# Norm, split and logits of three batches made during the last batch of attention

## The reference, cut to what matters

```
h = layernorm(x)                              # no weights
y = h + attn(layernorm(h, ln1_w, ln1_b))      # conv, q/k/v, rope, 16 heads, causal softmax, proj
z = layernorm(y, ln2_w, ln2_b)
expert = argmax(z @ router_w)                 # one of 4
out = y + (silu(z @ Wg[expert]) * (z @ Wv[expert])) @ proj[expert]
x = x + 0.5 * out
```

## Time and profile before

| | us |
|---|---|
| runs, median (lowest to highest) | 2196.71 (2192.24 to 2207.43), 3 runs |
| the profiled execution | 2191.62 |
| its span in the trace | 2189.9 |
| PE, DVE, ACT, POOL busy | 1866.5, 1437.3, 1302.0, 581.3 |

### The profile page before, as it was taken

The page is one execution under the profiler, slowest core; times in us unless marked ns, Lnnn a source line. Parts: engine busy times, 40 slices in busy tenths (PEclk is TensorE's granted clock), DMA queues, the critical chain, the costliest instruction groups (busy, mean ns, idle before and its releaser), DMA issues.

```text
span 2189.9 us, 23815 instructions
## 1 busy us (share of the span) xinstructions
PE 1866.5 (85%) x8305; PEld 1056.7 (48%) x8324; DVE 1437.3 (66%) x2318; ACT 1302.0 (59%) x2022; POOL 581.3 (27%) x685
## 2 busy tenths in 40 slices
PE   8999999999999989998677777997677677777998
PEld 6886444344434437885233334784122323332786
DVE  6886564456445647886755653886899755662787
ACT  6997555555555558997255556555644535556554
POOL 1443000000000002443522222222599612223221
PEclk9999999999999999999689998998799779999999
DMA  3221000000000002220000000200000000000110
GB/s 97 79 69 56 1 17 17 0 17 17 17 0 17 10 10 71 71 73 29 1 1 1 1 1 1 78 29 0 10 3 31 1 1 1 1 1 1 52 55 19
DMA packets 23746, 52.39 MB, mean 24 GB/s; under 512 B 2336, under 2 KB 6816, under 8 KB 23648
## 3 DMA queue, kind: packets, MB, share of 16 engines
q1 hardware_dynamic: 23648, 51.12, 7.3%
HBM read 49.47 MB, written 1.64 MB: 23 GB/s over the span
## 4 chain that ended last, share of the span: by engine, by line
PE 57%; DVE 21%; ACT 14%; issue 4%; POOL 2%; DMA 1%; ACTq 0%; POOLq 0%; DVEq 0%; SPq 0%
PE ps L440 9%; PE ps L442 9%; PE ps L441 9%; PE ps L708 5%; DVE arena L1463 5%; PE ps L225 4%; DVE arena L1208 4%; PE ps L701 4%; PE ps L928 3%; PE ps L898 3%; ACT rstd L242 2%; PE ps L887 2%; ACT arena L990 2%; ACT arena L1040 2%; ACT rstd L238 2%
## 5 line engine op out<-in xcount | busy, mean ns | idle before, releaser
L548 DVE TENSOR_TENSOR hid_lo<-arena,hid_hi 128x512 fp32r<-128x512 f32 x384 | 340.6, 900 | 67.1 <-ACT arena L498 64.7
L526 POOL TENSOR_TENSOR w_lo<-wslot,w_hi 128x512 fp32r<-128x512 f32 x56 | 77.5, 1389 | 759.4 <-DVE w_hi L543 759.4
L1208 DVE TENSOR_REDUCE arena<-ps 128x1 f32<-128x512 f32 (+3 forms) x352 | 213.2, 638 | 88.8 <-PE ps L902 85.7
L440 PE MATMUL ps<-x_hi,w_hi 128*128 128x512 f32 x512 | 208.1, 406 | 0.6 <-DVE arena L630 0.6
L441 PE MATMUL ps<-x_lo,w_hi 128*128 128x512 f32 x512 | 205.2, 401 | 0.0
L442 PE MATMUL ps<-x_hi,w_lo 128*128 128x512 f32 x512 | 205.0, 400 | 0.0
L495 ACT ACTIVATE hid_hi<-ps,wslot 128x512 fp32r<-128x512 f32 x256 | 177.1, 692 | 34.1 <-PE ps L442 6.3
L1040 ACT ACTIVATE arena<-ps 128x1024 f32<-128x1024 f32 (+3 forms) x256 | 166.5, 706 | 48.5 <-PE ps L918 47.9
L1126 POOL TENSOR_SCALAR_AFFINE_SELECT arena<-arena 128x256 f32<-128x256 f32 x256 | 102.2, 406 | 330.7 <-ACT arena L1040 328.2
L898 PE MATMUL ps<-arena 128*128 128x128 bf16 (+3 forms) x498 | 132.5, 332 | 65.3 <-DVE arena L1208 37.1
L498 ACT ACTIVATE arena<-ps,wslot 128x512 f32<-128x512 f32 x256 | 175.1, 684 | 0.0
(11 more groups left out here) (225 smaller groups left out, 3863.7 us busy)
## 6 DMA issues: line engine op xcount, KB each, us to landing
arena<-gates_dram SPq DMA_DIRECT2D x96, 256.0 KB, 3.5
wslot<-pack_a SPq DMA_DIRECT2D x16, 514.5 KB, 3.7
wslot<-pack_b SPq DMA_DIRECT2D x8, 901.5 KB, 4.6
wslot<-pack_c SPq DMA_DIRECT2D x8, 768.0 KB, 4.5
res<-x_in SPq DMA_DIRECT2D x4, 256.0 KB, 4.5
out_dram<-res SPq DMA_DIRECT2D x4, 256.0 KB, 2.9
bc_dram<-arena SPq DMA_DIRECT2D x1, 384.0 KB, 3.2
arena<-bc_dram SPq DMA_DIRECT2D x16, 24.0 KB
```

The lines of the kernel that those rows point to most:

```text
L440: pe.matmul(ps[:, bank, :], w1, hi, start=start, stop=False)
L548: dve.tensor_tensor(hid_lo[item % 2][:, k, :], hid32[:, k, :], hid_hi[item % 2][:, k, :].bitcast(F32), ALU.subtract).then_inc(S["hid_ok"], 1)
L1208: dve.tensor_reduce(neg_max[:, i, heads[0]:heads[-1] + 1:step], ps[:, bank, 0:len(heads) * keys].rearrange("p (m k) -> p m k", k=keys), AX ...
```

## The change

The norm of batches 0, 1 and 2 moves into batch 3 of attention. Each is spread over steps that begin at j = 2, 5 and 8 (`NORM_STEPS`): PE makes the mean behind the scores of step j+1 and the variance one step on; ACT squares behind the exponentials of step j, takes Ln and Exp one step on, and the high part three steps on; DVE centres at j, scales at j+2, and makes the low part at j+4. DVE now makes both parts of the weights of expert 0, at j = 0 to 2; POOL's part of that goes. The router products of batches 0 to 2 stand between the last turns and the last projection, in bank 5, and DVE copies their logits out ahead of the last `added_back`. Batch 3 is normed inside the experts' first item: its mean stands behind unit 0 on PE, its variance behind unit 2, its logits in unit 4, and ACT takes its square, Ln and Exp ahead of the first Silu. The gates are transposed at item 1, k = 3 instead of item 1, k = 0; DVE takes the rest of the router in unit 4 and the copy of the gates in unit 5. The counts of units, of products and of DMAs stay.

```diff
+        LATE = NB - 1
+        NORM_BANKS = [(5, 6)] * LATE + [(6, 7)]
+        EARLY_BANK, LATE_BANK = 5, 7
+        def pe_norm_mean(pe, c, t):
+            n, bank = c["ln"] + 2, NORM_BANKS[t][0]
+            pe.wait_ge(S["t_free"], att_x1(c, t))
+            if 0 < t < LATE:
+                pe.wait_ge(S["ln_xc"], 4 * n + t)
+            pe.matmul(ps[:, bank, :], mean_w, hb[:, t, :], start=True, stop=True).then_inc(S["ln_mean"], 1)
+        def pe_norm_var(pe, c, t):
+            pe.wait_ge(S["ln_sq"], 4 * n + t + 1)
...
+            pe.matmul(ps[:, bank, :], mean_w, sq[:, t, :], start=True, stop=True).then_inc(S["ln_var"], 1)
+        def act_norm_square(act, c, t):
+            act.wait_ge(S["ln_xc"], 4 * (c["ln"] + 2) + t + 1)
+            act.activation(sq[:, t, :], xc[:, t, :], ACT.Square).then_inc(S["ln_sq"], 1)
+        def act_norm_root(act, c, t):
+            act.wait_ge(S["ln_var"], 4 * n + t + 1)
+            act.activation(rstd[:, t, :], ps[:, NORM_BANKS[t][1], :], ACT.Ln, bias=eps).then_inc(S["ln_log"], 1)
+            act.wait_ge(S["ln_log"], 4 * n + t + 1)
+            act.activation(rstd[:, t, :], rstd[:, t, :], ACT.Exp, scale=-0.5).then_inc(S["ln_rs"], 1)
...
@@ dve_router (top == 1)
-                dve.tensor_copy(val, lg).then_inc(S["lg_read"], 1)
+                early = experts * TPB * LATE
+                dve.wait_ge(S["lg_early"], late + 1)
+                dve.tensor_copy(arena[:, 8192:8192 + early], ps[:, EARLY_BANK, 0:early]).then_inc(S["lg_part"], 1)
+                yield
+                dve.wait_ge(S["logits"], call + 1)
+                dve.tensor_copy(arena[:, 8192 + early:8192 + TILES * experts],
+                                ps[:, LATE_BANK, early:TILES * experts]).then_inc(S["lg_read"], 1)
                 dve.wait_ge(S["lg_read"], call + 1)
-                yield
+                dve.wait_ge(S["lg_part"], late + 1)
@@ pe_experts1
-                    if item == 1 and k == 0:
+                    if (item, k) == (0, 0):
+                        pe_norm_mean(pe, c, LATE)
+                    if (item, k) == (0, 2):
+                        pe_norm_var(pe, c, LATE)
+                    if (item, k) == (1, 0):
+                        pe_norm_logits(pe, c, LATE, LATE_BANK).then_inc(S["logits"], 1)
+                    if (item, k) == (1, 3):
                         pe_gates(pe, c["moe_call"], EXPERTS1)
@@ act_experts1
+            act_norm_square(act, c, LATE)
+            act_norm_root(act, c, LATE)
             for n in range(total + 1):
+                if n == 1:
+                    act_norm_high(act, c, LATE)
@@ dve_experts1
-            next(router)
+            dve_norm_centre(dve, c, LATE)
+            dve_norm_scale(dve, c, LATE)
...
-                if n in (0, 6):
+                if n == 2:
+                    dve_norm_low(dve, c, LATE)
+                if n == 4:
+                    next(router)
+                if n in (5, 8):
                     next(router, None)
@@ pe_attention, batch 3 (b + 1 == NB)
+        NORM_STEPS = [2, 5, 8]
+                    else:
+                        if j in NORM_STEPS:
+                            pe_norm_mean(pe, c, NORM_STEPS.index(j))
+                        if j - 1 in NORM_STEPS:
+                            pe_norm_var(pe, c, NORM_STEPS.index(j - 1))
                     values(b, j)
...
-            for m in range(3, TURNS):
-                turned(NB - 1, m)
+            turned(NB - 1, 3)
+            pe_norm_logits(pe, c, 0, EARLY_BANK)
+            turned(NB - 1, 4)
+            pe_norm_logits(pe, c, 1, EARLY_BANK)
+            pe_norm_logits(pe, c, 2, EARLY_BANK).then_inc(S["lg_early"], 1)
+            turned(NB - 1, 5)
@@ act_attention, batch 3
+                        if j in NORM_STEPS:
+                            act_norm_square(act, c, NORM_STEPS.index(j))
+                        if j - 1 in NORM_STEPS:
+                            act_norm_root(act, c, NORM_STEPS.index(j - 1))
+                        if j - 3 in NORM_STEPS:
+                            act_norm_high(act, c, NORM_STEPS.index(j - 3))
@@ dve_attention, batch 3
+                        if j < C_PIECES:
+                            dve_weights(dve, c, C_PIECES, 0, j)
+                        if j in NORM_STEPS:
+                            dve_norm_centre(dve, c, NORM_STEPS.index(j))
+                        if j < C_PIECES:
+                            cut = slice(SEQ * j, SEQ * j + SEQ)
+                            dve.wait_ge(S["w_hi_ok"], c["parts"] + j + 1)
+                            dve.tensor_tensor(w_lo[0][:, cut], wslot[:, 0, cut], w_hi[0][:, cut].bitcast(F32),
+                                              ALU.subtract).then_inc(S["w_parts"], 1)
+                        if j - 2 in NORM_STEPS:
+                            dve_norm_scale(dve, c, NORM_STEPS.index(j - 2))
+                        if j - 4 in NORM_STEPS:
+                            dve_norm_low(dve, c, NORM_STEPS.index(j - 4))
             normed(NB - 1, 3)
+            next(router)
             added_back(NB - 1)
```

More of the change, by code:

```diff
@@ L284, in act_ln_split, with dve_ln_split @@
             split(NB - 1)
-        def dve_ln_split(dve, n, src, affine, c, pieces):
+        def dve_ln_split(dve, n, src, c, pieces):
             for t in range(NB):
@@ L299, in dve_ln_split @@
                 dve.wait_ge(S["ln_rs"], 4 * n + t + 1)
[L300 to L307, removed]
+                dve.tensor_tensor(ha[:, t, :], xc[:, t, :], rstd[:, t, :], ALU.mult).then_inc(S["ln_out"], 1)
                 if t:
@@ new lines, in pe_norm_logits @@
+        def pe_norm_logits(pe, c, t, bank):
+            pe.wait_ge(S["ln_out"], 4 * (c["ln"] + 2) + t + 1)
+            for i in range(TPB * t, TPB * t + TPB):
+                mm = pe.matmul(ps[:, bank, EXPERTS1 * i:EXPERTS1 * (i + 1)], ha[:, t, (i % TPB) * P:(i % TPB + 1) * P],
+                               pcol("router"), start=True, stop=True)
+            return mm
+        def act_norm_square(act, c, t):
+            act.wait_ge(S["ln_xc"], 4 * (c["ln"] + 2) + t + 1)
+            act.activation(sq[:, t, :], xc[:, t, :], ACT.Square).then_inc(S["ln_sq"], 1)
@@ new lines, in act_norm_root, with act_norm_high @@
+        def act_norm_root(act, c, t):
+            n = c["ln"] + 2
+            act.wait_ge(S["ln_var"], 4 * n + t + 1)
+            act.activation(rstd[:, t, :], ps[:, NORM_BANKS[t][1], :], ACT.Ln, bias=eps).then_inc(S["ln_log"], 1)
+            act.wait_ge(S["ln_log"], 4 * n + t + 1)
+            act.activation(rstd[:, t, :], rstd[:, t, :], ACT.Exp, scale=-0.5).then_inc(S["ln_rs"], 1)
+        def act_norm_high(act, c, t):
+            act.wait_ge(S["ln_out"], 4 * (c["ln"] + 2) + t + 1)
+            act.activation(x_hi[:, t, :], ha[:, t, :], ACT.Copy).then_inc(S["x_hi_ok"], 1)
@@ new lines, in dve_norm_centre, with dve_norm_scale @@
+        def dve_norm_centre(dve, c, t):
+            dve.wait_ge(S["ln_mean"], 4 * (c["ln"] + 2) + t + 1)
+            dve.tensor_tensor(xc[:, t, :], hb[:, t, :], ps[:, NORM_BANKS[t][0], :],
+                              ALU.subtract).then_inc(S["ln_xc"], 1)
+        def dve_norm_scale(dve, c, t):
+            n, m = c["ln"] + 2, c["lns"] + 1
+            dve.wait_ge(S["ln_rs"], 4 * n + t + 1)
+            dve.scalar_tensor_tensor(out=ha[:, t, :], in0=xc[:, t, :], scalar=pcol("ln2_w"), in1=rstd[:, t, :],
+                                     op0=ALU.mult, op1=ALU.mult).then_inc(S["ln_scaled"], 1)
+            dve.wait_ge(S["ln_scaled"], 4 * m + t + 1)
+            dve.tensor_scalar(ha[:, t, :], ha[:, t, :], pcol("ln2_b"), None, ALU.add).then_inc(S["ln_out"], 1)
@@ L333, in build, with dve_router @@
         chain = [0]
-        def dve_router(dve, call, exp_call, experts, top):
+        def dve_router(dve, call, exp_call, experts, top, late=0):
             def link(ins):
@@ L347, in dve_router @@
             desc = ccol("desc8" if experts == 8 else "desc4").unsqueeze(1).to_broadcast([P, TILES, experts])
-            dve.wait_ge(S["logits"], call + 1)
-            lg = ps[:, LOGIT_BANK, 0:TILES * experts].rearrange("p (t e) -> p t e", e=experts)
             val = tile3(0)
             if top == 2:
+                dve.wait_ge(S["logits"], call + 1)
+                lg = ps[:, LOGIT_BANK, 0:TILES * experts].rearrange("p (t e) -> p t e", e=experts)
                 link(dve.tensor_reduce(rs[0], lg, AX_X, ALU.max))
@@ L453, in pe_down @@
                     pe.wait_ge(S["gate_cp"], c["moe_call"] + 1)
+                if banks == 2 and item == 0:
+                    pe.wait_ge(S["ln_xc"], 4 * (c["ln"] + 2) + NB)
             pe.wait_ge(S["hid_ok"], 4 * (base + item) + k + 1)
@@ L529, in pool_experts @@
         def pool_experts(pool, c, dst, experts, pieces, lag):
-            pool_weights(pool, c, pieces, 0)
+            if experts == EXPERTS0:
+                pool_weights(pool, c, pieces, 0)
             for item in range(NB * experts + lag):
@@ L1152, in dve_conv, with dve_attention @@
```

(4 more changed lines are left out.)

24 lines of the change are left out of this document (16 added, 8 removed).

## The result

The changed kernel takes 2225.75 us (median of 4 runs, 2223.35 to 2227.82) against 2202.07 us before (4 runs, 2192.24 to 2208.88), a ratio of 1.0111 (95% interval 1.0063 to 1.0158). Forecast were 2206 us and a range of 2188 to 2222. It is slower, on the side that was forecast: by 24 us between these medians, where the prediction had added 12 us to the profiled run.

A forecast was written before the change was run, and what follows sets the result against it. Bound: a serial chain of small pieces, 18.8 us between attention and experts, twice. Per stage +14.5 - 11.9 + 3.4 = +6.0, +12.0 for two, giving 2203.6 from 2191.6; with half of 5.1 us carried, 2206; range 2188 to 2222.

The forecast's parts named there:

- Term 1: Batch 3 of attention gets 14.5 us longer per stage: 18.9 for three norms, less 4.4 of old ACT waits absorbed.
- The bound of 20.2: Upper bound for batch 3's lengthening per stage, if PE is at half clock for each of the six norm products.
- The sign that I gave: What would show the forecast right in batch 3 of attention: it lasts 44 us instead of 29.7.
- Term 2: From the last turn of attention to unit 3 of the experts: 11.9 us shorter per stage.
- my bound: Last turn to unit 3: -10.3 us if the eight later router products also run at half clock.
- Terms 2 and 3: Per stage: last turn to unit 3 of the experts, -11.9 us; then units 3 to 11, +3.4 us.
- both halves of the term: Units 3 to 11: gates copied out 2.1 us later; half clock after PE's stand loses about 2.6 us.
- The fast one: Batch 3: gaps take the norm work, lengthening it only 3.2 us per stage; whole kernel 2181 us; 9%.
- The clock rival: Batch 3: PE's granted clock falls under 0.7, +17 us per stage, whole kernel 2225 us; 9%.
- The POOL rival: Batch 3: DVE's added operations hold up POOL's masks, and these PE; stage +15 us, whole 2222 us; 4%.

The follow-up runs named there:

- e1: The kernel before, run and traced once more with no edit: 2199.4 us, ratio 0.9999.
- e2: The changed kernel with ACT's and PE's pieces of the three norms, and DVE's scaling and low part, put at later steps: 2203.01 us, ratio 1.0018.
- e9: The changed kernel with three idle products on PE behind the values of steps 2, 3, 5, 6, 8 and 9 of batch 3: 2218.87 us, ratio 1.0093.
- e4: The changed kernel with the transpose of the gates at item 1, k = 1 instead of k = 3: 2219.79 us, ratio 1.0093.
- e3: The changed kernel with three idle products on PE behind the values of every step of batch 3: 2223.33 us, ratio 1.0100.

## Why the prediction was wrong, step by step

*Baseline.* The sum stood on a profiled run of 2191.6, of which I carried 2.5 us to the median. The median of the runs of before is 2202.07 in the comparison and 2198.5 to 2199.1 in the three later ones. The forecast stood on 2194.1, so 4 to 8 us of the missed 20 are the footing, and e1 shows what most of it is: where the half clock falls in batches 0 to 2.

*Term 1, batch 3 (forecast +14.5, measured +18.4 per stage): this is the step that failed.* Its mechanism was right: ACT stands in its own order for the centring and the variance, and e2, which changes only that order, gave 10 us per stage back. Its size was off in three parts, two of them put too low. I had ACT absorb 4.4 us of its old waits; of the 7.3 us of idle time that the window had before, 5.7 are still there (19.0 less the 13.3 of new waits), so 1.6 were absorbed: those before step 2 and at the end of the batch stay or grow. The waits for centring were 9.0 us, not the 6.8 of my sum, which had 2.27 for each norm at full clock. With the projection of batch 2, which I had left out, ahead of the scores but at full clock, the middle norm's wait was 2.50; where the half clock lay on the projection it was 4.05, and in the second stage it lay ahead of the first norm and made that wait 3.71. So most of the 2.2 us is the half clock, and little of it the place of the projection. I had set the clock to its old 0.94 and it fell to 0.82; e9, which raised it to 0.92, took 1.4 to 2.5 us off the batch. And ACT's work grew by 6.9, not 7.6, since consecutive operations overlap a little. In sum 2.8 + 2.2 - 0.7, less 0.3 on the variance, is 4.0, against 3.9 measured. The bound of 20.2 held. The sign that I gave, 44 us for the batch, belongs to the longer window of the earlier trace rows; in the window used here it is 42.9, against 46.8.

*Term 2 (forecast -11.9).* Measured from the last turn to unit 3: -11.1 in the first stage (30.49 to 19.38) and -12.7 in the second (to 17.82). That the two average to the forecast is in part luck: the projection began 6.2 us after the turn in the first stage (forecast 4.2; all twelve router products ran at half clock, and my bound had eight of them), and the mean of batch 3 held PE for 0.5 us, not the 1.7 that I gave it. The chain behind was right: from the variance to unit 3 it took 5.09 us (forecast 5.05), with a stand of 4.07 (forecast some 4). In it the table load was 1.28 us and Silu began 1.30 us after the load's start, as in the earlier trace rows. The 2.66 us that the Trainium skill gives for a switch (ScalarE: Activation LUTs, What ACT_TABLE_LOAD costs) would have shown here as a further 1.4 us of waiting, and there is none.

*Terms 2 and 3 together (forecast -8.5).* Start of val of unit 8 after the last copy-out: 46.6 us before (46.2 to 47.0 in four windows), 39.4 and 38.3 after, so -7.2 and -8.3, about -7.7; the last val of the experts is earlier by as much. From unit 3 at 1383.66 to unit 11, which val of unit 8 releases, the changed kernel took 20.0 us against 16.5, and 20.4 against 16.1 in the second stage: +3.6 and +4.4 where +3.4 was forecast. The gates were copied out 13.3 us after unit 3 (forecast 11.1). The clock did fall after the stand (granted 0.50 from 1383.6 to 1388.6), so both halves of the term came, where I had taken the middle; e4 gave the gates' part back.

*Sum.* 18.4 - 7.7 = +10.7 us per stage, +21 for two, against +24 between the medians; forecast was +12. The 2 to 3 us between them are within the chance of batches 0 to 2.

*The rivals.* The fast one (gaps take it) is what e2 approaches: with most of the waits gone batch 3 is 8.2 us longer than before, not 3.2, since hardly any of ACT's work went into the old gaps. The clock rival was given 9% with a threshold of 0.7 and 2225 us. The time was reached with a clock of 0.82, so it is not this rival, with its threshold, that came true, though a part of its mechanism did. The POOL rival, priced at 9.1 us, had at most half a microsecond of PE's waits in the window. The rule of the Trainium skill on the shared port pair (SBUF — State Buffer, SBUF: two separate sides) agrees roughly with the masks that took 1.20 instead of 0.77 us: the rule, by which the first of them would be blocked until w_lo ended at 1314.86, gives an estimate of 1.34. It prices a collision, and this one cost ACT nothing.

The range, 2188 to 2222, ended 4 us short. It was made around a low footing, and the upper tail of term 1 was given too little: its own bounds (3.2 to 20.2) were wide, and I gave the clock a separate and small chance instead of a part in every case. That the sign was right rests on the mechanism; that the time was missed by only 1% does not speak for the sum, whose term 1 was low in each stage by a fifth of what was measured.

## What to carry to other kernels

When work is moved beside other work, the free share of an engine is not the price; in an engine that keeps its order, the price of a moved piece is what stands between it and its input on every other engine's list at that place. Put each piece one hand-over later than its input can be there: here that was worth 1% of the kernel, with what the clock gave back by it. Price the pieces with the clock that the new waits leave, not with the old one. And take the footing from several traces of the kernel before, not from one, when the forecast is of the size of the run-to-run spread.

## What the runs showed of the hardware

Two lengths of the same unchanged stretch, 187.8 us at a granted clock of 0.95 and 193.0 at 0.90, occurred within one execution (e1). Over 1364.3 to 1371.5, the turns, router products and projection after batch 3, PE is busy without a gap and the granted clock is 0.53, the 1.2 GHz level nearly throughout; with the idle products in the batch before it (e3) it was 0.78 in the like stretch:

```profile
1364.28:1371.50 7.22, 7.22 (x34) 6.70 (x35) 0.76 (x3) 0.60 (x1) 0.00 (x0) 0.53 0.00 0
...
1383.60:1388.60 5.00, 4.94 (x12) 3.88 (x13) 4.38 (x8) 2.93 (x6) 0.00 (x0) 0.50 0.00 0
```

```profile
1365.00:1372.00 7.00, 7.00 (x40) 5.75 (x41) 1.44 (x4) 0.60 (x1) 0.00 (x0) 0.78 0.01 2
```
